# Cross-attention on one core: wo, gamma and four x tiles loaded ahead of slot 0, and five smaller moves

## The reference

```python
Q = (query @ w_q.T).reshape(B, S, NUM_HEADS, D_K).transpose(0, 2, 1, 3)      # query = x
K = (key @ w_k.T).reshape(B, -1, NUM_HEADS, D_K).transpose(0, 2, 1, 3)       # key = value = ctx
V = (value @ w_v.T).reshape(B, -1, NUM_HEADS, D_K).transpose(0, 2, 1, 3)
scores = jnp.einsum('bhqd,bhkd->bhqk', Q, K) / np.sqrt(D_K)
attn = jax.nn.softmax(scores, axis=-1)
ctx = jnp.einsum('bhqk,bhkd->bhqd', attn, V)
out = ctx.transpose(0, 2, 1, 3).reshape(B, S, D_MODEL) @ w_o.T + b_o
x = out + query
mu = jnp.mean(x, axis=-1, keepdims=True)
var = jnp.mean(jnp.square(x - mu), axis=-1, keepdims=True)
return (x - mu) * jax.lax.rsqrt(var + LN_EPS) * ln_gamma + ln_beta
```

## Time and profile before

| | |
|---|---|
| median of 3 runs | 559.24 us (558.02 to 559.49) |
| the profiled execution | 559.06 us |
| its span | 557.3 us |
| busy, share of the span | PE 96%, PEld 66%, DVE 83%, ACT 71%, POOL 76% |
| the chain that ended last | PE 81%, DVE 6%, DMA 4%, SyncE's queue 3% |
| DMA | 63.23 MB, mean 113 GB/s |

### The profile page before, as it was taken

How to read it: one execution, slowest core, us unless ns; L and a number is a source line. 1 busy time by engine, 2 the same in 40 slices (tenths; PEclk the granted TensorE clock), 3 DMA queues, 4 the chain that set the end, 5 groups by cost and what they waited for, 6 DMA issues and landing times.

```text
span 557.3 us, 12699 instructions
## 1 busy us (share of the span) xinstructions
PE 533.4 (96%) x4522; PEld 365.2 (66%) x4522; DVE 465.2 (83%) x874; ACT 393.8 (71%) x733; POOL 424.5 (76%) x391
## 2 busy tenths in 40 slices
PE   8988889999999999999999999999999999998991
PEld 6755556766676666766676667666676667665561
DVE  7867658888888888988889888988888888988785
ACT  7636667777777777777777777777777777766662
POOL 1714778888888888888888888888888888776665
PEclk9999999999999999999999999999999999999996
DMA  8434552443344334442343334443343432322122
GB/s 303 150 86 132 147 162 70 131 129 95 95 130 131 102 91 125 130 123 84 113 133 109 120 95 125 107 123 100 120 121 98 133 103 84 85 67 72 44 76 95
DMA packets 74111, 63.23 MB, mean 113 GB/s; under 512 B 46528, under 2 KB 46528, under 8 KB 74048
## 3 DMA queue, kind: packets, MB, share of 16 engines
q1 hardware_dynamic: 74048, 62.42, 37.5%
HBM read 39.58 MB, written 16.78 MB: 101 GB/s over the span
## 4 chain that ended last, share of the span: by engine, by line
PE 81%; DVE 6%; DMA 4%; SPq 3%; issue 2%; POOL 2%; ACT 1%; DVEq 0%; POOLq 0%
PE ps_q L408 28%; PE ps_o L414 27%; PE ps_c L370 9%; PE ps_s L343 7%; DMA max_rows<-max_turned 4%; PE ps_s L353 3%; PE ps_q L281 2%; SPq L215 2%; PE ps_s L281 2%; PE ps_o L281 2%; DVE half_max L701 1%; DVE turned L696 1%; POOL y L877 1%; PE ps_c L288 1%; POOL y L875 1%
## 5 line engine op out<-in xcount | busy, mean ns | idle before, releaser
L408 PE MATMUL ps_q<-x_hi,wq_lo 64*128 64x512 f32 x448 | 186.8, 417 | 1.7 <-DVE values L666 1.6
L414 PE MATMUL ps_o<-wo_hi,c_lo 64*128 64x512 f32 x448 | 186.7, 417 | 0.0
L408 PE MATMUL ps_q<-x_hi,wq_hi 64*128 64x512 f32 x448 | 175.7, 392 | 0.0
L408 PE MATMUL ps_q<-x_lo,wq_hi 64*128 64x512 f32 x448 | 175.5, 392 | 0.0
L414 PE MATMUL ps_o<-wo_hi,c_hi 64*128 64x512 f32 x448 | 175.2, 391 | 0.0
L414 PE MATMUL ps_o<-wo_lo,c_hi 64*128 64x512 f32 x448 | 174.8, 390 | 0.0
L408 PEld LDWEIGHTS ps_q<-x_hi,wq_lo 64*128 64x128 f32 x448 | 82.4, 184 | 70.9 <-DVE z L745 45.3
L875 POOL TENSOR_TENSOR y<-y,gamma_row 128x512 f32<-128x512 f32 x60 | 77.6, 1294 | 58.9 <-ACT y L560 58.9
L847 POOL TENSOR_TENSOR x_lo<-xT_raw,x_hi 128x512 fp32r<-128x512 f32 x60 | 77.6, 1293 | 27.4 <-ACT x_hi L495 25.3
L853 POOL TENSOR_TENSOR c_lo<-c_raw,c_hi 128x512 fp32r<-128x512 f32 x64 | 82.7, 1292 | 17.3 <-ACT c_hi L495 17.2
L414 PEld LDWEIGHTS ps_o<-wo_hi,c_hi 64*128 64x128 f32 x448 | 82.6, 184 | 10.6
(11 more groups left out here) (104 smaller groups left out, 1114.5 us busy)
## 6 DMA issues: line engine op xcount, KB each, us to landing
xT_raw<-in_xT SPq DMA_DIRECT2D x64, 256.0 KB, 3.3
x_raw<-in_x SPq DMA_DIRECT2D x64, 256.0 KB, 2.9
out<-y SPq DMA_DIRECT2D x64, 256.0 KB, 2.4
max_rows<-max_turned SPq DMA_DIRECT2D x256, 16.0 KB
ctx_raw<-in_ctxT SPq DMA_DIRECT2D x4, 256.0 KB, 4.5
wk_raw<-in_wkT SPq DMA_DIRECT2D x4, 256.0 KB, 4.7
wq_raw<-in_wqT SPq DMA_DIRECT2D x4, 256.0 KB, 5.9
wv_raw<-in_wvT SPq DMA_DIRECT2D x4, 256.0 KB, 6.9
```

Of the source, the lines that this page charges most:

```text
L408: return nc.tensor.matmul(ps_q[:, 0, :], w[l][half, k, dims], x_[r][half, qc % 2, k, :], start=(half is lower and k == 0 and step == 0), s ...
L414: return nc.tensor.matmul(ps_o[:, 0, :], cx[l][half, k, tile], wo[r][half, k, :], start=(half is upper and k == 0 and step == 0), stop=(ha ...
```

## The change

Six edits. SyncE issues all of wo, the bias, gamma, beta and x tiles 0 to 3 before slot 0's maxima, and one x tile a slot in slots 2 to 5 (tiles 4 to 7). On TensorE `subtract_max` stands ahead of `project_values` in slots 1 to 3, and there are 8 warm-up matmuls for 10. On VectorE `odd_values` of slot 6 stands ahead of `turn_max`, and in slot 62 `turn_max(61)` stands right behind the fold. ScalarE makes the shifts of tiles 59 to 61 in two operations, where GpSimd made them in one. The small tensors are allocated behind the large ones, so that the places of the large ones are multiples of 64 bytes.

```diff
--- before.py
+++ after.py
@@ -24,7 +24,7 @@
     OUT_LAG = 7
     SPLIT_AHEAD = 5
     BY_VECTOR = (57, 58, 62, 63)
-    WARM = 10
+    WARM = 8
     SCALE = float(DK) ** -0.5
     EPS = 1e-5
     assert CHUNKS == 2 * BATCHES and 2 * KEYS == P and KT * P == DM and TILES == SLOTS and DK == 32
@@ -69,7 +69,6 @@
         signs = sb("signs", [P, 2, KEYS], fp32)
         select = sb("select", [P, P], fp32r)
-        eps_column = sb("eps_column", [P, 1], fp32)
         xT_raw = sb("xT_raw", [P, KT, CHUNK], fp32)
         x_hi, x_lo = sb("x_hi", [P, 2, KT, CHUNK], fp32r), sb("x_lo", [P, 2, KT, CHUNK], fp32r)
@@ -77,19 +76,12 @@
         turned = sb("turned", [P, 2 * CHUNK], fp32)
-        half_max = sb("half_max", [P, 2, 32], fp32)
-
-        max_hl, max_turned = sb("max_hl", [P, 3, 32], fp32r), sb("max_turned", [P, 2, 32], fp32)
-
         max_rows = sb("max_rows", [P, 2, CHUNK], fp32r)
         probs = sb("probs", [P, 2, 2, CHUNK], fp32)
         inverse, c_raw = sb("inverse", [P, CHUNK], fp32), sb("c_raw", [P, CHUNK], fp32)
         x_raw = sb("x_raw", [P, 8, DM], fp32)
-        stats = sb("stats", [P, 8, 6], fp32)
-        mean_var = sb("mean_var", [P, 8, 2], fp32)
-        log_var, rstd, shift = (sb(n, [P, 8], fp32) for n in ("log_var", "rstd", "shift"))
         with ExitStack() as raw:
@@ -101,6 +93,16 @@
             c_hi[odd] = sb(f"c_hi{odd}", [P, G, CHUNK], fp32r)
             c_lo[odd] = sb(f"c_lo{odd}", [P, G, CHUNK], fp32r)
+        half_max = sb("half_max", [P, 2, 32], fp32)
+        max_hl, max_turned = sb("max_hl", [P, 3, 32], fp32r), sb("max_turned", [P, 2, 32], fp32)
+        stats = sb("stats", [P, 8, 6], fp32)
+        mean_var = sb("mean_var", [P, 8, 2], fp32)
+        log_var, rstd, shift = (sb(n, [P, 8], fp32) for n in ("log_var", "rstd", "shift"))
+        eps_column = sb("eps_column", [P, 1], fp32)
         def ps(name, banks):
             return ctx.enter_context(nc.psum_tensor(name, [P, banks, 512], fp32))
@@ -152,6 +154,7 @@
         log_var_done, rstd_done, shift_done, normed_done, scaled_done, y_done = (
             sem(n) for n in ("log_var_done", "rstd_done", "shift_done", "normed_done", "scaled_done", "y_done"))
         last_scaled_done, last_y_done = sem("last_scaled_done"), sem("last_y_done")
+        mean_negated_done = sem("mean_negated_done")
         def key_blocks(t, s, j):
@@ -198,8 +201,6 @@
             for u in range(KT, SPLIT_AHEAD + 3):
                 sp.wait_ge(x_lo_done, u - KT + 1)
                 load_xT(u)
-            sp.wait_ge(keys_zeroed, 2)
-            sp.wait_ge(keys_lo_done, G)
             def load_x(i):
                 wait(sp, z_done, i - 7)
@@ -237,24 +238,25 @@
                     sp.wait_ge(y_done, by_scalar(i) + 1)
                 sp.dma_start(out[P * i:P * (i + 1), :], y[:, i % 4, :]).then_inc(y_stored[i % 4], 16)
+            for k in range(KT):
+                for head in range(2):
+                    sp.dma_start(wo_raw[64 * head:64 * (head + 1), k, :],
+                                 woT_v[k, :, :].rearrange("(p h d) n -> h p d n", p=2, h=2)[head, :, :, :]
+                                 ).then_inc(wo_loaded[k], 16)
+            sp.dma_start(bias_row[:, :], b_o.partition_broadcast(P)).then_inc(bias_loaded, 16)
+            for row, src in ((gamma_row, gamma), (beta_row, beta)):
+                sp.dma_start(row[:, :], src.partition_broadcast(P)).then_inc(gains_loaded, 16)
+            for i in range(4):
+                load_x(i)
+            sp.wait_ge(keys_zeroed, 2)
+            sp.wait_ge(keys_lo_done, G)
             for t in range(OUT_LAG):
                 fill_max_rows(t)
                 load_ahead(t)
-
-                if 1 <= t <= KT:
-
-                    for head in range(2):
-                        sp.dma_start(wo_raw[64 * head:64 * (head + 1), t - 1, :],
-                                     woT_v[t - 1, :, :].rearrange("(p h d) n -> h p d n", p=2, h=2)[head, :, :, :]
-                                     ).then_inc(wo_loaded[t - 1], 16)
-                if t == 1:
-                    sp.dma_start(bias_row[:, :], b_o.partition_broadcast(P)).then_inc(bias_loaded, 16)
                 if 2 <= t <= 5:
-                    load_x(2 * t - 4)
-                    load_x(2 * t - 3)
-                if t == 5:
-                    for row, src in ((gamma_row, gamma), (beta_row, beta)):
-                        sp.dma_start(row[:, :], src.partition_broadcast(P)).then_inc(gains_loaded, 16)
+                    load_x(t + 2)
                 next_keys(t)
             load_ahead(OUT_LAG)
@@ -447,11 +449,13 @@
             for t in range(OUT_LAG):
                 score(t)
                 project_queries(t + 1)
+                if 1 <= t <= 3:
+                    subtract_max(t - 1)
                 if t == 0:
                     project_values(0, second_half)
                 else:
                     project_values((t + 1) // 2, first_half if t % 2 else second_half)
-                if 1 <= t < OUT_LAG - 1:
+                if 3 < t < OUT_LAG - 1:
                     subtract_max(t - 1)
                 if t >= 2:
                     combine_values(t - 2)
@@ -559,6 +563,15 @@
                 wait(act, y_stored[s], 16 * (i // 4))
                 nc.scalar.activation(y[:, s, :], z[:, s, :], ACT.Identity, bias=shift[:, c:c + 1],
                                      scale=rstd[:, c:c + 1]).then_inc(normed_done, 1)
+            def shift_mean(i):
+                c = i % 8
+                nc.scalar.activation(shift[:, c:c + 1], mean_var[:, c, 0:1], ACT.Identity, scale=-1.0
+                                     ).then_inc(mean_negated_done, 1)
+                act.wait_ge(mean_negated_done, by_scalar(i) - by_scalar(59) + 1)
+                act.wait_ge(rstd_done, i + 1)
+                nc.scalar.activation(shift[:, c:c + 1], shift[:, c:c + 1], ACT.Identity, scale=rstd[:, c:c + 1]
+                                     ).then_inc(shift_done, 1)
             def exponentiate(n):
                 act.wait_ge(shifted_done, n + 1)
@@ -642,12 +655,10 @@
             invert_deviation(57)
             context_to_hi(63)
             invert_deviation(58)
-            invert_deviation(59)
-            normalise(59)
-            invert_deviation(60)
-            normalise(60)
-            invert_deviation(61)
-            normalise(61)
+            for i in (59, 60, 61):
+                invert_deviation(i)
+                shift_mean(i)
+                normalise(i)
             invert_deviation(62)
             invert_deviation(63)
@@ -770,11 +781,14 @@
                 if t >= 3:
                     divide(t - 3)
                 queries_to_lo(t + 1)
+                if t == OUT_LAG - 1:
+                    odd_values(t // 2)
                 turn_max(t)
-                if t % 2 == 0:
+                if t % 2 == 0 and t < OUT_LAG - 1:
                     odd_values(t // 2)
-            for t in range(OUT_LAG, SLOTS - 1):
+            for t in range(OUT_LAG, SLOTS - 2):
                 i = t - OUT_LAG
                 if i >= 1:
                     turn_scores(t - 1)
@@ -789,6 +803,14 @@
                 queries_to_lo(t + 1)
+            turn_scores(61)
+            half_maxima(61)
+            fold_halves(61)
+            turn_max(61)
+            divide(59)
+            statistics(54)
+            add_residual(55)
+            queries_to_lo(63)
             statistics(55)
             turn_scores(62)
             half_maxima(62)
@@ -915,7 +937,6 @@
             scale(56)
             context_to_lo(63)
             for i in (59, 60, 61):
-                shift_mean(i)
                 scale(i)
```

## The result

The changed kernel takes 570.3 us (median of 5 runs, 569.51 to 571.69) where the kernel before took 559.49 beside it (558.02 to 560.62): a ratio of 1.0194, 95% interval 1.0171 to 1.0217. The forecast was 568.6 in 562 to 574. The profiled execution is the slowest of the five, 571.69 us (span 569.8), so the two profiled executions stand 12.63 us apart.

The account below looks back on a forecast made before the run. TensorE was taken to bound the main loop, busy 439.7 of 440.3 us, leaving only head and tail to change. From the profiled 559.06 us: +12.9 head, -1.1 and -2.3 tail, giving 568.6; range 562 to 574.

Parts of the forecast that it names:

- The rate of wo, and its two engines: Loads ahead of slot 0: two engines serve each wo DMA, so 1.05 MB at 49 GB/s takes 21.4 us.
- the two late parts of the maxima: Slot 0: the maxima use eight engines, wo's two among them, so they wait until wo is through; TensorE stands still 17.6 us.
- The landing at 48.0: Head: slot 0's maxima land at about 48.0 us, bounds 44 and 51; before, TensorE took them at 32.22.
- the 0.8 us for the maxima behind them: Head: time for slot 0's maxima to land after the loads ahead are through at 47.3; some 0.8 us.
- rival C: Head: the stall echoes, SyncE is held up, slots 2 to 4 wait 1 to 2 us each again; 573 us, chance 0.17.
- The clock, 2.1 us: Head: after the wait TensorE restarts at the lower clock level, costing 2.1 us, bounds 0 and 3.
- What the head gives back: Slots 1 to 6 after the landing: shorter waits from the reordering and moved loads; main loop starts at about 86.5.
- The gain without a stall: Head: without the stall the changes would gain some 5.9 us, 3.5 of it in slots 4 and 5.
- +12.9: Head: the main loop's start, 73.63 before, moves to about 86.5, 12.9 us later.
- The 64-byte places at 0: Whole kernel: moving the small tensors touches no wait; 0, bounds -1 and +1 us.
- WARM 8 worth nothing: Start: 8 warm-up matmuls bring score(0) 0.35 us earlier, worth nothing here because it lies ahead of the stall.
- The tail, -1.1 and -2.3: Tail: maxima 61 turned early save 1.1 us (0.5 to 1.7); ScalarE's own shifts save 2.3 (1.5 to 3).

Follow-up runs that it names:

- all but wo: The changed kernel with wo's DMAs put back into slots 1 to 4; 552.08 us, 0.9864 of the kernel before.
- wo alone ahead: The changed kernel with only wo ahead of slot 0, in 4 DMAs, and bias, gamma, beta and x in later slots; 550.4 us, 0.9832 of the kernel before.
- kept-warm: The changed kernel with 76 more matmuls on TensorE in the stop, in slot 1 before subtract_max(0); 567.89 us, 1.0127 of the kernel before.

## Why the prediction was right

**The rate of wo, and its two engines.** Right. 49 GB/s and 0.13 came back as 53 and 0.14 (51 without one fetch of 16 KB of instructions that falls in the window); by whole rows, with the other loads, it was 248 GB/s and most of the stop went. The sign of the change hung on this alone. The step from the two late parts of the maxima to the stop held as well, as the packets show.

**The landing at 48.0.** It came at 49.8, inside 44 to 51. The loads were through at the two engines at about 47.8, where 47.3 was forecast; the mis-sized term is the 0.8 us for the maxima behind them, which took 2.0. Their last quarter moved from 47.8 to 49.0 with packets of the xT tile and the keys between. About half of the 1.8 us varies: in the two other kernels with the same loads ahead TensorE went on at 49.17 and 48.90. SyncE, too, was held up, as rival C had it: it was to be through at 26, and 8 issues took it 13.45 us and the maxima's four 5.88, until 44.54. But this did not move the landing: in each window of 1 us from 22 to 49 the DMA share is 0.13 or more, two engines' worth, so no gap shows for which SyncE was too late. C's price did not come either: no slot behind waited again.

**The clock, 2.1 us.** It was 2.6, within 0 to 3.

**What the head gives back.** From the landing to the first paired matmul 38.5 us were forecast and 39.83 measured: the clock's 0.5, 0.6 in slots 2 and 3, 0.1 in 4 and 5, 0.1 in slot 6. With the landing's 1.8 that is the difference between +12.9 and +16.0, to rounding. The gain without a stall, put at 5.9, shows where only wo stands ahead in 4 DMAs: 4.8, and 0.8 of wait is left there.

**The 64-byte places at 0.** Probably wrong, and it was a step of argument: I read the same 417 ns in both products and took that for the absence of an effect. The mean of one instruction, rounded to 1 ns, can't show 0.015 us of a slot of 7.84; the length of the slot could. Measured were -2.2 us alone and -2.1 on top of the tail edits, outside my bounds of 1; the shorter slots account for 0.5 to 1.5, and the sorting of runs by clock leaves 1.1, which is at the bound. In the changed kernel the slot is 7.832 against 7.845, some 0.7 us, of which a second long slot takes much back (-0.25 in all).

**WARM 8 worth nothing.** Right here, behind the stall. By itself, where 0.35 had been put, no run can tell: the interval holds both.

**The tail, -1.1 and -2.3.** It measured -1.19 (the scores of slot 63 against z of tile 55) and -2.07, in sum -3.26 against -3.4; all but wo has -3.25 and wo alone ahead -3.27. The last passes of VectorE cost 1.56 and 1.43 beside GpSimd, as allowed for.

By the profiled executions it came out at +12.6 where +9.5 was forecast: 3.1 of stall and head too little, little else. The median, 570.3, was 1.7 over the forecast; that it comes so near is in part luck, since the profiled execution, on which the sum was checked, was the slowest of five. The number alone does not tell the forecast from rival C (573); that no slot behind the stop waits does.

## What to carry to other kernels

Before a load is moved ahead of a critical small transfer, ask how many DMA engines it uses and what follows it on the same ones. The busy share times 16, in a window where it is alone, tells the number; if it is two, change the form of the DMA before its place. An issuer of its own is no way past, since the transfers meet in the engines. And what a move of small tensors to other addresses does is to be read from the length of a repeated slot, not from the rounded means of single instructions.

## What the runs showed of the hardware that I had not expected

**The clock's first rise varies from execution to execution.** The same eight warm-up matmuls, in the changed kernel and in the kept-warm one:

```profile
1.98 3.78 PE L290 MATMUL ps_c<-kbd_hi 128*128 128x512 f32 x8 [1.98 <-DVE kbd_hi L685]
5.68 0.77 PE L283 MATMUL ps_s<-ctx_hi,wk_lo 128*128 128x512 f32 x1
6.25 0.63 PE L283 MATMUL ps_s<-ctx_lo,wk_hi 128*128 128x512 f32 x1
```
```profile
1.99 3.78 PE L291 MATMUL ps_c<-kbd_hi 128*128 128x512 f32 x8 [1.99 <-DVE kbd_hi L689]
5.63 0.49 PE L284 MATMUL ps_s<-ctx_hi,wk_lo 128*128 128x512 f32 x1
5.96 0.39 PE L284 MATMUL ps_s<-ctx_lo,wk_hi 128*128 128x512 f32 x1
```

Up to here the two programs are the same. In the one the granted clock rises at 8.0 (the starts stay 0.43 us or more apart until then), in the other at 5.67. Over the fourteen profiled executions it rises between 5.7 and 8.1: in the seven with ten matmuls at 5.9 to 8.1, in the seven with eight at 5.7 to 8.1. The ranges are the same; with one profile of each kernel, an effect of the number is not excluded.

**It can fall behind a short wait.** With wo by whole rows in the kernel before, TensorE waits 1.68 us for maxima in the tail, and the passes behind it start every 0.43 us instead of 0.23. The profile of WARM 8 alone shows the same behind the same wait:

```profile
512.60 0.49 PE L354 MATMUL ps_s<-max_rows,select 64*128 64x512 f32 x2 [1.68 <-DMA max_rows<-max_turned]
...
513.81 0.63 PE L282 MATMUL ps_o<-wo_hi,c_hi 128*128 128x512 f32 x1
514.24 0.63 PE L282 MATMUL ps_o<-wo_hi,c_lo 128*128 128x512 f32 x1
```
```profile
515.51 0.50 PE L353 MATMUL ps_s<-max_rows,select 64*128 64x512 f32 x2 [1.70 <-DMA max_rows<-max_turned]
```

From 513.5 to 516.5 (and from 516.2 to 519.5 in the other) the granted clock is 0.50. In the profiled execution of the kernel before the same wait of 1.70 left it at full speed, and so did waits of 1.90 and 1.98 in the head. From this wait's end to TensorE's next wait it takes 10.15 us with the drop (512.60 to 522.75) and 8.63 without (515.63 to 524.26 before): it costs 1.5 us. Of the six profiled kernels with the old tail three have such a drop (these two, and wo issued by ScalarE, behind 1.71 us); of the eight in which maxima 61 are turned earlier, so that the wait is gone, none has. What decides among the six is open. This is perhaps why the tail edits alone earn 3.7 us by the medians and 2.1 by the profile. Their six runs lie within 0.9 us, where 17 of the kernel before beside them spread over 5.8; but with the places too, six runs spread over 2.7, so the wait is not all of the scatter.
